# Two halves for x and C by turns, a convolution tap by ScalarE a step ahead, the second within-chunk sum and the copies of the sum's parts placed ahead

## The reference

```python
zxbcdt = h @ Wi                                   # z 256, xBC 512, dt 8 columns
xp = jnp.pad(xBC, ((0, 0), (3, 0), (0, 0)))
conv = cb + sum(xp[:, k:k + L, :] * cw[:, k] for k in range(4))
xBC = silu(conv)
xs, Bm, Cm = split(xBC)                           # 256, 128, 128
dt = softplus(dt + dtb); A = -exp(Alog)
# scan over the tokens t, for every head:
hs = hs * exp(dt * A)[t] + (dt * xs)[t] * B[t]
y  = hs @ C[t]
y = rmsnorm((y + D * xs) * silu(z), gw)
h = h + y @ Wo
```

## Time and profile before

| | |
|---|---|
| median of 3 runs | 1199.43 us (1195.77 to 1206.58) |
| the profiled execution | 1199.3 us |
| its span, first to last instruction | 1197.3 us |
| busy, share of the span | VectorE 84%, TensorE 83%, ScalarE 73%, GpSimd 56% |
| mean granted TensorE clock | 0.956 |

### The profile page before, as it was taken

The page is one execution under the profiler, slowest core; times in us unless marked ns, Lnnn a source line. Parts: engine busy times, 40 slices in busy tenths (PEclk is TensorE's granted clock), DMA queues, the critical chain, the costliest instruction groups (busy, mean ns, idle before and its releaser), DMA issues. The chain is left out here.

```text
span 1197.3 us, 25713 instructions
## 1 busy us (share of the span) xinstructions
PE 992.9 (83%) x6136; PEld 560.2 (47%) x6136; DVE 1000.5 (84%) x1833; ACT 870.8 (73%) x1692; POOL 675.6 (56%) x853
## 2 busy tenths in 40 slices
PE   5688888888888988888888988886688876999980
PEld 4244444444444444444444444443344444777760
DVE  6689999999999999988998889985588775888865
ACT  5588888888888888888888888886465653565540
POOL 0177567766777567655666466553154351566661
PEclk9699999999999999999999999999788897999995
DMA  5111233222322232200000010000010014766737
GB/s 137 33 33 32 85 133 103 83 86 100 134 85 83 84 135 101 75 24 25 23 24 21 23 28 21 23 16 1 1 36 32 26 36 142 232 232 213 236 120 210
DMA packets 85579, 97.80 MB, mean 82 GB/s; under 512 B 20698, under 2 KB 65888, under 8 KB 85536
## 3 DMA queue, kind: packets, MB, share of 16 engines
q1 hardware_dynamic: 80544, 88.83, 23.4%
q0 software_dynamic: 4992, 8.48, 2.1%
HBM read 59.67 MB, written 37.83 MB: 81 GB/s over the span
## 5 line engine op out<-in xcount | busy, mean ns | idle before, releaser
L1331 DVE SCALAR_TENSOR_TENSOR cv<-bank,PAR,cv 128x511 f32<-128x511 f32 (+2 forms) x384 | 273.7, 740 | 11.6 <-DVE cv L1327 4.3
L1347 DVE SCALAR_TENSOR_TENSOR M<-E,bank 128x512 f32<-128x512 f32 x256 | 168.4, 679 | 28.5 <-PE bank L549 16.6
L1657 POOL TENSOR_TENSOR yt<-yt,ti 128x384 f32<-128x384 f32 x64 | 64.2, 1003 | 225.2 <-DVE ti L1448 225.2
L931 ACT ACTIVATE E<-bank 128x512 f32<-128x512 f32 x256 | 149.4, 597 | 48.4 <-DVE M L1347 47.5
L481 PE MATMUL bank<-hn,WA 128*128 128x512 f32 x256 | 145.2, 650 | 42.7 <-DVE cv L1331 42.0
L1688 POOL DMA_INDIRECT RS<-y,XR x92 | 98.6, 1072 | 79.1 <-DVE y L1545 55.5
L1681 POOL DMA_INDIRECT XS<-stage,IDX x64 | 65.0, 1016 | 77.0 <-DVE run L1306 52.8
L1079 ACT ACTIVATE hr<-bank,W1B 128x512 f32<-128x512 f32 x92 | 63.5, 690 | 57.1 <-PE bank L671 53.3
L1062 ACT ACTIVATE xbc<-cv 128x512 f32<-128x512 f32 x128 | 76.9, 624 | 37.3 <-DVE yt L1443 36.4
L549 PE MATMUL bank<-M,dtx 128*32 128x128 f32 x2048 | 82.5, 278 | 21.8 <-DVE o_sb L1366 15.8
L1475 DVE TENSOR_TENSOR hL<-hr,hH 128x512 fp32r<-128x512 f32 x124 | 87.3, 704 | 4.3
(11 more groups left out here) (244 smaller groups left out, 2638.6 us busy)
## 6 DMA issues: line engine op xcount, KB each, us to landing
XS<-PADT SPq DMA_DIRECT2D x32, 520.0 KB, 4.0
WA<-w_in SPq DMA_DIRECT2D x192, 64.0 KB, 1.8
W1B<-WD SPq DMA_DIRECT2D x23, 514.0 KB, 3.4
W2B<-WD SPq DMA_DIRECT2D x23, 512.5 KB, 4.9
WD<-WS SPq DMA_DIRECT2D x16, 512.0 KB, 2.7
XR<-XS SPq DMA_DIRECT2D x23, 260.0 KB, 4.5
RW<-w_in SPq DMA_DIRECT2D x18, 256.0 KB, 4.2
WO_raw<-w_out SPq DMA_DIRECT2D x32, 128.0 KB, 3.3
```

What stands on the lines that cost most here:

```text
L931: f(E[i % 2][:, :], bank[2 + i % 2][:, :], ACT.Exp).then_inc(e_a, 1)
L1331: stt(out=cv[t][:, s:L], in0=src[:, 0:L - s], scalar=PAR[:, bass.ds(cw + 3 - s, 1)], in1=cv[t][:, s:L], op0=ALU.mult, op1=ALU.add).then_in ...
L1347: stt(out=M[i % 4][:, :].rearrange("p (n t) -> p n t", n=4), in0=E[i % 2][:, :].rearrange("p (n t) -> p n t", n=4), scalar=1.0, in1=bank[5 ...
```

## The change

`xbc[X0]`, `xbc[X1]` and `xbc[TC]` get two halves, and step k writes half k mod 2 (`conv_rows`); ScalarE's SiLUs wait for the readers of step k - 2 in place of k - 1. The loop runs over pairs of steps, since the half must be known where the instruction is written: 14 turns of two bodies in place of 28 turns of one. `tap(1, 0)` leaves VectorE; ScalarE makes it at the end of body k for step k + 1 (`early_tap`), once before step 0. `within(1)` stands ahead of the mean of squares on TensorE. SyncE's seven copies from `p2` stand ahead of the load of `WA[5]`.

```diff
@@ -120,7 +120,7 @@
         WO_raw = sb("WO_raw", 2 * DM)
         sqh, lnm, rB, hn = sb("sqh", L), sb("lnm", L), sb("rB", L), sb("hn", L)
         cv = [sb(f"cv{t}", L) for t in range(4)]
-        xbc = [sb(f"xbc{t}", L) for t in range(4)]
+        xbc = [sb(f"xbc{t}", L if t == TB else 2 * L) for t in range(4)]
         zraw = sb("zraw", 2 * L)[:, 0:L]
         u, ax, ex, ln1 = sb("u", P), sb("ax", P), sb("ex", P), sb("ln1", P)
         dt_, dA, cum, r1 = sb("dt_", P), sb("dA", P), sb("cum", P), sb("r1", P)
@@ -224,33 +224,41 @@
         ra_in = [sem(f"ra{b}_in") for b in range(NB)]
         fin_sum, fin_gb, fin_o = sem("fin_sum"), sem("fin_gb"), sem("fin_o")
 
+        def pairs_of_steps(eng, body, first, last, **kw):
+
+            with eng.Fori(first // 2, last // 2) as i:
+                for odd in (1, 0):
+                    k = eng.snap(2 * i + (2 - odd))
+                    body(k, odd, A=True, B=True, C=True, N=True, **kw)
+
         def steps(eng, body):
 
 
-            body(0, A=True, B=False, C=False, N=True)
-            body(1, A=True, B=True, C=False, N=True)
-            body(2, A=True, B=True, C=True, N=True)
-            with eng.Fori(3, STEPS - 1) as k:
-                body(k, A=True, B=True, C=True, N=True)
-            body(STEPS - 1, A=True, B=True, C=True, N=False)
-            body(STEPS, A=False, B=True, C=True, N=False)
-            body(STEPS + 1, A=False, B=False, C=True, N=False)
+            body(0, 0, A=True, B=False, C=False, N=True)
+            body(1, 1, A=True, B=True, C=False, N=True)
+            body(2, 0, A=True, B=True, C=True, N=True)
+            pairs_of_steps(eng, body, 3, STEPS - 1)
+            body(STEPS - 1, 1, A=True, B=True, C=True, N=False)
+            body(STEPS, 0, A=False, B=True, C=True, N=False)
+            body(STEPS + 1, 1, A=False, B=False, C=True, N=False)
 
...
+        def conv_rows(t, odd, at=0, n=L):
+
+            first = 0 if t == TB else odd % 2 * L
+            return xbc[t][:, first + at:first + at + n]
 
         def scattered(eng, n):
 
@@ -308,11 +316,14 @@
                     sp.dma_start(WO_raw[:, :], rows(w_out, at_j, 2 * DM)).then_inc(s_wo, 16)
                 if N:
                     at = [sp.snap((k + 1) // NB * (6 * P * P) + t * P * P) for t in range(6)]
-                for t in range(6):
-                    if N:
-
-                        wait(sp, pj_mm, 6 * k + t + 1)
-                        sp.dma_start(WA[t][:, :], rows(w_in, at[t], P)).then_inc(wa[t], 16)
+                def next_projection(t):
+
+                    wait(sp, pj_mm, 6 * k + t + 1)
+                    sp.dma_start(WA[t][:, :], rows(w_in, at[t], P)).then_inc(wa[t], 16)
+
+                if N:
+                    for t in range(5):
+                        next_projection(t)
                 if A:
 
                     if B:
@@ -325,6 +336,8 @@
                         sp.dma_start(PC[q:q + 24, :], p2[q:q + 24, :]).then_inc(p4_in, 16)
                     for c in range(1, NC):
                         sp.dma_start(P4[:, c * CH:(c + 1) * CH], p2[32 * c:32 * c + 32, :]).then_inc(p4_in, 16)
+                if N:
+                    next_projection(5)
                 if W == "up" or W == "down":
                     first = sp.snap((k - 3) * P)
                     wait(sp, split_p, 2 * k)
@@ -597,6 +610,7 @@
                 if B:
                     rows_of_heads(1)
                     decays(3)
+                    within(1)
                 if B and not A:
                     square_mean_of_m(0)
                 if N:
@@ -606,8 +620,6 @@
                 elif A:
                     wait(pe, zc_a, k + 1)
                     square_mean_of_h(0)
-                if B:
-                    within(1)
                 if A:
                     project(5)
 
@@ -922,7 +934,15 @@
                 wait(act, rt_v, 20 * (n - 1) + 1)
                 f(pr[:, :], second_bank(n)[:, 0:32], ACT.Exp, scale=-1.0).then_inc(ex_a, 1)
 
-            def body(k, A, B, C, N):
+            def early_tap(n):
+
+                first = act.snap(n // NB * NPAR)
+                wait(act, pj_mm, 6 * n + 2)
+                wait(act, silu_a, 6 * (n - 1) + SILU_TURN[1] + 1)
+                f(cv[1][:, :], bank[1][:, :], ACT.Identity, scale=PAR[:, bass.ds(first + C_CW + 4 + 3, 1)],
+                  bias=PAR[:, bass.ds(first + C_CB + 1, 1)]).then_inc(tap_v[1], 1)
+
+            def body(k, odd, A, B, C, N):
                 j, i2 = k - 1, k - 2
 
                 def decay_exp(i):
@@ -1056,10 +1076,10 @@
                         if t == TB:
                             wait(act, t_mm, 4 * k)
                         elif t == TC:
-                            wait(act, yi_mm, 2 * k)
+                            wait(act, yi_mm, 2 * (k - 1))
                         else:
-                            wait(act, fin_v, 4 * (k - 1) + 1 + t)
-                        f(xbc[t][:, :], cv[t][:, :], ACT.Silu).then_inc(silu_a, 1)
+                            wait(act, fin_v, 4 * (k - 2) + 1 + t)
+                        f(conv_rows(t, odd), cv[t][:, :], ACT.Silu).then_inc(silu_a, 1)
 
                     wait(act, pj_mm, 6 * k + 6)
                     wait(act, fin_p, 4 * (k - 1))
@@ -1070,6 +1090,8 @@
                     silu(X0)
                     silu(X1)
                     silu(TC)
+                if N:
+                    early_tap(k + 1)
 
 
             def relu(q, t, bias):
@@ -1145,6 +1167,7 @@
                 if i > 0:
                     result(q - 1, W2B[(i - 1) % 2][:, 2 * HE:2 * HE + 1].bitcast(F32))
 
+            early_tap(0)
             steps(act, body)
             act.wait_ge(hup, NB + STEPS)
             put_tokens(0)
@@ -1371,7 +1394,6 @@
                 if A:
                     tap(0, 0)
                     tap(0, 1)
-                    tap(1, 0)
                     tap(0, 2)
                     tap(1, 1)
                     tap(0, 3)
@@ -1440,7 +1462,7 @@
                         if t == 0:
                             wait(dve, y_mm, 4 * j + 4)
                         wait(dve, fin_p, 4 * j - 2 + 2 * t)
-                        stt(out=yt[t][:, :], in0=xbc[t][:, :], scalar=PAR[:, bass.ds(pj + C_D + t, 1)],
+                        stt(out=yt[t][:, :], in0=conv_rows(t, odd + 1), scalar=PAR[:, bass.ds(pj + C_D + t, 1)],
                             in1=bank[6 + t][:, :], op0=ALU.mult, op1=ALU.add).then_inc(fin_v, 1)
                     for t in range(2):
                         wait(dve, yi_mm, 2 * j + 1 + t)
```

More of the change, by code:

```diff
@@ L239, in steps_with_weights @@
-        def steps_with_weights(eng, body):
[L242 to L253, removed]
+        def pairs_of_steps(eng, body, first, last, **kw):
[3 more added lines that the diff above has]
+                    body(k, odd, A=True, B=True, C=True, N=True, **kw)
@@ new lines, in steps @@
+        def steps(eng, body):
+            body(0, 0, A=True, B=False, C=False, N=True)
[5 more added lines that the diff above has]
+            body(STEPS + 1, 1, A=False, B=False, C=True, N=False)
+        def steps_with_weights(eng, body):
+            body(0, 0, A=True, B=False, C=False, N=True)
+            body(1, 1, A=True, B=True, C=False, N=True, W="shared")
+            body(2, 0, A=True, B=True, C=True, N=True, W="shared")
+            pairs_of_steps(eng, body, 3, 3 + NE, W="up")
+            pairs_of_steps(eng, body, 3 + NE, 3 + 2 * NE, W="down")
+            pairs_of_steps(eng, body, 3 + 2 * NE, STEPS - 1)
+            body(STEPS - 1, 1, A=True, B=True, C=True, N=False)
+            body(STEPS, 0, A=False, B=True, C=True, N=False)
+            body(STEPS + 1, 1, A=False, B=False, C=True, N=False)
@@ L294, in _, with body @@
                          allow_slow_non_contiguous=True).then_inc(unit_out, 16)
-            def body(k, A, B, C, N, W=None):
+            def body(k, odd, A, B, C, N, W=None):
                 if W:
@@ L514, in turn @@
                         ins = nc.tensor.transpose(bank[TURN_BANK[c]][:, n * P:(n + 1) * P],
-                                                  xbc[t][:, c * CH:(c + 1) * CH], ident)
+                                                  conv_rows(t, odd + 1, c * CH, CH), ident)
                     ins.then_inc(t_mm, 1)
@@ L559, in body @@
                         cs = slice(c * CH, (c + 1) * CH)
-                        ins = mm(bank[5][:, cs], xbc[TB][:, cs], xbc[TC][:, cs], start=True, stop=True)
+                        ins = mm(bank[5][:, cs], xbc[TB][:, cs], conv_rows(TC, odd + 1, c * CH, CH), start=True, stop=True)
                     ins.then_inc(g_mm, 1)
@@ L645, in body @@
                             cs = slice(c * CH, (c + 1) * CH)
-                            ins = mm(bank[2 + t][:, cs], S[c][:, t * P:(t + 1) * P], xbc[TC][:, cs], start=True, stop=True)
+                            ins = mm(bank[2 + t][:, cs], S[c][:, t * P:(t + 1) * P], conv_rows(TC, odd + 1, c * CH, CH), start=True, stop=True)
                         ins.then_inc(yi_mm, 1)
```

## The result

The changed kernel takes **1159.32 us** (median of 4 runs, 1159.04 to 1162.99) against 1199.65 us (4 runs, 1195.77 to 1206.58): a ratio of 0.9665, 95% interval 0.9616 to 0.9713. The profiled execution took 1162.99 us around a span of 1161.0; against the 1197.3 us of before that is 36.3 us. Of these, 2.8 lie ahead of the loop (its first tap at 99.91, before at 102.72), 32.3 in the loop, and 1.2 behind it. The two outer stretches differ between kernels by more than that: over the 13 traces of this case the loop begins between 96.4 and 103.1 us, and 405.9 to 414.5 us lie behind it. A part is therefore best priced by the loop.

What follows compares the result with a forecast made beforehand. It took a step to be bound by VectorE from `ti` to `tap(3,3)`, then by TensorE back to `ti`. Gains of 18.8, 6.3 and 2.0 us, together 27.1, took 1199.3 to 1172.2 us; range 1160 to 1189 us.

Steps and rivals of the forecast that it cites:

- The tap: Moving `tap(1,0)` from VectorE to ScalarE gains 0.48 us a step net, with bounds of 0 and 0.72.
- The boundary in a pair: Between the two steps of a loop turn no branch remains: 0.45 us for 14 of 28 boundaries, 6.3 us.
- The copies: SyncE's copies ahead of the load of `WA[5]` gain nothing by themselves, at most 0.1 us.
- The written-out steps: Steps 1, 2 and 31, outside the loop, gain 0.67 us each, 2.0 us together.
- The sum ahead of the mean: `within(1)` before the mean on TensorE gains 0.19 us a step, at `within(2)`; bounds 0 and 0.27.
- ScalarE's tap at no cost: The new tap at ScalarE's step end, covered by SiLUs starting 1.18 us earlier, costs 0.
- its safety net: Without that cover, 0.7 us more on ScalarE would still meet TensorE's 0.89 us wait for `tap(0,3)`.
- Rival 3: The longer loop body is fetched anew each turn: 4 us a turn, 56 us, 1228 us; chance 0.05.
- Rival 4: A covered wait replaces the tap: no change, 1195 to 1200 us, chance 0.06; sign: a later logarithm after the mean.
- Rival 2: All bounds fall well: the tap pair costs nothing extra, VectorE keeps its 0.27; 37 us gained, 1162 us; chance 0.04.
- Rival 1: Only the tap removed from VectorE counts: 31 x 0.48 = 14.9 us gained, 1184 us; chance 0.15.

Runs made afterwards that it cites:

- experiment 5: The kernel before with only `within(1)` moved ahead of the mean of squares: 1188.5 us, ratio 0.9902.
- Experiments 1: The changed kernel with `within(1)` put back behind the mean of squares on TensorE: 1178.81 us, ratio to the kernel before 0.9822.
- experiment 9: The changed kernel with single buffers for x and C and the old waits, early tap kept: 1180.25 us, ratio to the kernel before 0.9849.
- experiment 2: The changed kernel with the first tap of X1 back on VectorE, halves kept: 1183.84 us, ratio to the kernel before 0.9859.
- experiment 8: The kernel before with `within(1)` ahead of the mean and GpSimd's split of the expert weights behind `own_rows`: 1187.35 us, ratio 0.99.
- experiment 7: The kernel before with only GpSimd's split of the expert weights moved behind `own_rows`: 1200.86 us, ratio 1.0.

## Why the prediction was off

**The tap: right.** Booked at 0.48 us a step; the segment up to `o_sb` fell by 0.47 and by 0.51 to 0.57, and rose by 0.48 when the tap went back.

**The boundary in a pair: right.** Booked at 0.45 for 14 boundaries; 0.37 became -0.08, with the pairs alone as with all parts.

**The copies: right**, 0. **The written-out steps: not shown as a sum.** 2.0 us were booked. 2.8 went ahead of the loop and 1.2 behind it, but both stretches vary by more from kernel to kernel, and ahead of the loop the granted clock is at its lower level for parts of steps 0 and 1, which went 2.3 us down and 1.4 up. Step 2, at the full clock in both, fell by 1.15 us (23.88 to 22.73), where 0.67 was booked.

**The sum ahead of the mean: the step that failed.** The prediction said that "`project(5)` still starts at 436.87" behind `tap(3,3)`, and that only 0.19 us could be won, at `within(2)`. It read that from step 16, a weights step, and took it for all 28. For such a step it holds: in experiment 5 the weights steps gained just these 0.19 us (13.08 to 12.89), since `spend`, held up by GpSimd, made `tap(3,3)` end as late as the mean and the sum had. In the 12 later steps of the loop `spend` takes 0.23 us, `tap(3,3)` is done 0.67 us before `project(5)`, and what `project(5)` and `apply_decay(5)` wait for is `within(1)`. That stood behind the mean, which waited 0.24 us for ScalarE's `zraw` while the sum could have run.

With the sum in that gap the segment from `o_sb` to `ti` went from 13.08 to 12.48 us. By the two TensorE timelines above, mean and sum begin 0.32 us earlier (3.04 us behind the start of `o_sb`, not 3.36) and take 0.06 less (1.54, not 1.60), so that `project(5)` begins 0.38 us earlier; and `within(2)`, whose `M` is now made in time, gains 0.23 more, the booked term. So 12 later steps gave 7.2 us. In the changed kernel `spend` takes 0.50 us in the 8 second weights steps, which gave 4.6, and 0.97 in the 8 first ones, which gave 0.6: 12.4 us in place of 28 x 0.19 = 5.3. Experiments 1 and 5 show it from TensorE's side.

With the other terms, 28 x 0.48 + 14 x 0.45 + 12.4 is 32.1 us, of the 32.3 measured in the loop. The median moved by 40.3 us and the two profiled executions by 36.3. The 4 us between lie in the spread: the profiled execution of the changed kernel was the slowest of its four. So of the 13 us by which the gain passed the sum, 7 are this term, 4 the spread, and 2 lie outside the loop. The slowest of the four runs (1162.99) lies inside the range, so which side of its edge the median fell on is chance; the term is wrong either way.

**ScalarE's tap at no cost: right, its safety net wrong.** "If the cover were gone, 0.7 us more on ScalarE would still meet those 0.89 us" is refuted by experiment 9: `sqy` and the projection of y hang on ScalarE too, and without the cover the time rises by 21 us.

**The rivals.** Rival 3 (code fetched at each turn): from 100 to 750 us the instruction queues moved 9 packets, 6 before:

```profile
q8 instruction: 3, 0.05, 0.0%
q14 instruction: 6, 0.05, 0.0%
```

The doubled bodies are held. Rival 4's sign is there, since the mean, and the logarithm with it, now come later, and `M` for the last heads waits 0.52 us for ScalarE's `E`; but it is done at 607.53 (606.84 + 0.69 on VectorE), and `within(3)`, which needs it, starts at 608.82 behind other matmuls. Rival 2 (1162) was nearest in its number, by another route: it let the tap's pair cost nothing, which the 0.48 of experiment 2 refutes, and gave the sum 0.27. Rival 1 left the sum and the boundary out.

**What the weights steps lost.** The 0.52 us by which the first weights steps stay behind the later ones was in no rival. `spend` had been held in the kernel before as well (0.86 us), but there the longer chain over the mean and the sum hid it; the shorter chain uncovered it.

## What to carry over

Read the bound of a segment in a step of every kind before you multiply by the number of steps: here `tap(3,3)` ended just ahead of `project(5)` in step 16, and 0.67 us ahead of it in steps 19 to 30, because GpSimd's program differed. Then look for an engine that has work queued and waits for an input ahead of it. Parts of such a change are not a sum: taken back one by one the sum, the tap and the second buffers lengthened the loop by 13.1, 22.5 and 19.9 us, where all parts together had shortened it by 32.3; alone the pairs and the sum shortened it by 5.8 and 10.3. The second buffers gained nothing at the boundary; their worth is to keep ScalarE's early tap from coming late. When VectorE is near the bound, look which of its instructions with two SBUF inputs start while GpSimd runs, and give GpSimd's movable work a wait that puts it beside instructions that read PSUM.

## What the runs showed of the hardware that I had not expected

- A VectorE instruction that starts beside a running GpSimd instruction can last beyond that one's end. In the loops `spend` took 0.23 us alone and up to 1.18 held (experiment 2), ending 0.04 us behind GpSimd's; the scan 0.41 at the least and up to 0.90, most often 0.28 behind; `hn` 0.75 and up to 1.56 (experiment 8), 0.55 behind. `M` (0.65 to 0.69), the taps, `yt` and `ti`, with a bank as an input, were never held.
- The granted clock can fall inside a loop whose steps are all alike: in 5 of 28 steps of experiment 2, in 2 of experiment 7 and in 1 of experiment 9, and in none of the other ten traces. The segment up to `o_sb` then took 1.1 us more (0.7 in experiment 9). Ahead of it TensorE had waited up to 1.59, 0.76 and 1.18 us, as it did in the neighbouring steps, where the clock stayed.
